# Softmax row sums in spare PSUM columns of the score banks, and a score bank that is refilled after the reciprocals instead of after the exponentials

## The reference, cut to what matters

```
x  = x + attention(groupnorm(x))
xn = layernorm(...)                                   # per position, 32 channels
scores = einsum('biqhd,bikhd->bihqk', q, k) + tri_bias + mask_bias    # 96 rows i, 4 heads, 96x96
a  = softmax(scores, axis=-1)
o  = einsum('bihqk,bikhd->biqhd', a, v)
out = einsum('bijk,ck->bijc', o * sigmoid(...), wo) + bo
```

## Time and profile before

| | |
|---|---|
| median of three runs | 320.16 us |
| the profiled execution | 320.25 us |
| its span (first to last record) | 318.4 us, so 1.85 us lie around it |
| PE busy, share of the span | 248.8 us (78%) |
| DVE busy | 241.3 us (76%) |
| ACT busy | 218.5 us (69%) |
| POOL busy | 128.0 us (40%) |
| attention pipeline | about 59 to 226 us of the span |

### The profile page before, as it was taken

One profiled execution on the slowest core, in us unless ns is written; L12 is line 12 of the kernel. 1 busy time (PEld: TensorE's weight loads), 2 busy tenths in 40 slices (PEclk: granted clock), 3 DMA queues, 4 the chain that ended last, 5 costly groups with the idle time before them and its releaser, 6 DMA issues.

```text
span 318.4 us, 7162 instructions
## 1 busy us (share of the span) xinstructions
PE 248.8 (78%) x2296; PEld 200.1 (63%) x2296; DVE 241.3 (76%) x543; ACT 218.5 (69%) x986; POOL 128.0 (40%) x140
## 2 busy tenths in 40 slices
PE   0597750589999999999999999998755977758710
PEld 0587320467778777887788787776555656658710
DVE  6058950578899888998989988887349479968994
ACT  1546650399998999998999989997445755426700
POOL 6670000045455455544554454555000365630562
PEclk9999595599999999999999999999758799978775
DMA  9100132635344354433544333410000462000017
GB/s 140 32 0 2 50 71 35 234 138 198 125 162 155 106 185 165 152 128 130 182 151 171 128 127 123 146 38 2 2 0 0 170 250 78 3 0 2 0 21 127
DMA packets 44041, 31.29 MB, mean 98 GB/s; under 512 B 23108, under 2 KB 44004, under 8 KB 44004
## 3 DMA queue, kind: packets, MB, share of 16 engines
q1 hardware_dynamic: 43004, 30.70, 30.5%
q10 hardware_dynamic: 1000, 0.13, 0.3%
HBM read 1.38 MB, written 1.18 MB: 8 GB/s over the span
## 4 chain that ended last, share of the span: by engine, by line
PE 64%; DVE 15%; DMA 6%; ACT 5%; issue 5%; SPq 2%; DVEq 0%; ACTq 0%
PE psum L1083 10%; PE psum L1135 10%; PE psum L1146 9%; PE psum L1086 5%; PE psum L1084 5%; PE psum L1115 5%; DMA maps<-mask_parts 4%; DVE tok L781 3%; PE psum L1001 3%; PE psum L979 2%; PE psum L1103 2%; PE psum L1204 2%; PE psum L1123 2%; DVE tok L836 2%; DMA maps<-in_x 2%
## 5 line engine op out<-in xcount | busy, mean ns | idle before, releaser
L497 POOL TENSOR_TENSOR probs<-probs,rden 96x384 f32<-96x384 f32 x96 | 79.0, 823 | 122.4 <-DVE rden L919 122.4
L645 ACT ACTIVATE probs<-psum,neg_max 96x96 f32<-96x96 f32 x384 | 124.1, 348 | 2.4 <-PE psum L1135 0.5
L645 ACT ACTIVATION_READ_ACCUMULATOR probs<-psum,neg_max 96x1 f32 x384 | 82.5, 215 | 0.0
L913 DVE COPY probs_t<-psum 96x384 f32<-96x384 f32 x96 | 52.9, 551 | 20.2 <-PE psum L1135 18.8
L882 DVE TENSOR_REDUCE neg_max<-psum 96x4 f32<-96x384 f32 x96 | 50.8, 529 | 2.0 <-PE psum L1086 2.0
L1083 PE MATMUL psum<-u_st,x_stack 128*96 128x384 f32 x96 | 40.5, 422 | 14.5 <-DMA u_st<-u_split 13.8
L1135 PE MATMUL psum<-ident,probs 96*96 96x96 f32 x384 | 47.7, 246 | 1.1 <-DVE probs_t L913 0.9
L1135 PEld LDWEIGHTS psum<-ident,probs 96*96 96x96 f32 x384 | 37.7, 126 | 5.4 <-issue 1.4
L1146 PE MATMUL psum<-probs_t,v_sb 128*32 128x96 f32 x768 | 35.8, 258 | 0.0
L1083 PEld LDWEIGHTS psum<-u_st,x_stack 128*96 128x96 f32 x96 | 15.7, 164 | 28.2 <-issue 14.0
L1086 PE MATMUL psum<-bias_lo,ident_r 128*96 128x384 f32 x96 | 33.0, 343 | 0.0
(11 more groups left out here) (167 smaller groups left out, 492.9 us busy)
## 6 DMA issues: line engine op xcount, KB each, us to landing
u_st<-u_split SPq DMA_DIRECT2D x96, 192.0 KB
x_stack<-shared SPq DMA_DIRECT2D x40, 96.0 KB, 2.1
x_stack<-bias_lo SPq DMA_DIRECT2D x10, 192.0 KB, 2.3
x_stack<-u_st SPq DMA_DIRECT2D x10, 192.0 KB, 2.3
maps<-in_x SPq DMA_DIRECT2D x4, 288.0 KB, 5.4
out_y<-maps SPq DMA_DIRECT2D x12, 96.0 KB, 2.2
x_stack<-shared SPq DMA_DIRECT2D x4, 192.0 KB, 2.3
bias_lo<-maps SPq DMA_DIRECT2D x24, 12.0 KB
```

Source lines behind the costliest of these rows:

```text
L497: pool.tensor_tensor(probs[:, m % SLOTS], probs[:, m % SLOTS], rden[:, m, :].unsqueeze(2).to_broadcast([N, H, N]), ALU.mult).then_inc(prob ...
L645: e = act.activation(probs[:, m % SLOTS, h], bank_s[m % 4][0:N, h * N:(h + 1) * N], ACT.Exp, bias=neg_max[:, m, h:h + 1], accum_out=den[:, ...
L913: dve.tensor_copy(probs_t[0:N, (m - T_BEHIND) % 2].rearrange("p h q -> p (h q)"), bank_t[0:N, 0:H * N]).then_inc(t_ready, 1)
```

## The change

`den` goes away. The row sums of row m are written to the four columns behind the scores, 384 to 387, of the same PSUM bank, and the reciprocals read them there. Since the bank now holds the row sums too, new scores may go into it only when the reciprocals of its last row are done, so PE waits for `rden_ready` where it waited for `exp_done`. The same count is used in the wait of the raw transposes behind the loop.

```diff
-        den = sb("den", [N, BODY, H])
...
+        def den_of(m):
+
+            return bank_s[m % 4][0:N, H * N:H * N + H]
...
-                                       ACT.Exp, bias=neg_max[:, m, h:h + 1], accum_out=den[:, m, h:h + 1])
+                                       ACT.Exp, bias=neg_max[:, m, h:h + 1],
+                                       accum_out=den_of(m)[:, h:h + 1])
...
-                    dve.reciprocal(rden[:, at, :], den[:, at, :]).then_inc(rden_ready, 1)
+                    dve.reciprocal(rden[:, at, :], den_of(at)).then_inc(rden_ready, 1)
...
-                need(pe, exp_done, BODY * r + m - 3)
+                need(pe, rden_ready, BODY * r + m - 3)
...
-                    pe.wait_ge(exp_done, s - 3)
+                    pe.wait_ge(rden_ready, s - 3)
```

## The result

The change makes the kernel slower: 365.83 us, the median of four executions (365.58 to 372.61), against 320.61 us in the same comparison. The ratio is 1.142 with a 95% interval of 1.137 to 1.146. The forecast was 367 us in a range of 361 to 378. Medians here are over all executions of a kernel, ratios over those near its fastest. The profiled execution took 365.63 us with a span of 363.8 us; its counterpart before took 320.25 us.

A forecast was written before the change was run, and what follows sets the result against it. PE was taken to pace the attention loop; the new wait makes PE and DVE take turns, 8.77 us per four steps against 6.70. 320.25 + 46.3 (loop) + 0.3 (start) = 366.9, stated as 367 us, range 361 to 378.

The forecast's parts named there:

- Piece 1: On PE, scores' start to transposes' start: 0.91, 1.48, 0.60, 0.78 us for n=0 to 3, together 3.77 per four steps.
- piece 4: Reciprocals' start to the start of whoever waits for them: 0.24 us, seen on POOL and taken for PE too.
- Pieces 2 and 3: PE transposes' start to DVE copy's start, 0.54 us, then copy's start to reciprocals' start, 0.47 us.
- The rival of the slow release: PE starts 0.15 us after DVE's end instead of 0.08, with a slower PSUM read: 373 to 379 us; chance 17%.
- The group: Four steps of the attention loop: 3.77 + 4 x 1.25 = 8.77 us against 6.70 before.
- The sum: 89 steps from the seventh scores take 195.1 us against 148.8, +46.3; with the start's +0.3 the total is 366.9 us.
- DVE at n=0: The tightest place: DVE's other work puts the copy 1.45 us behind the reciprocal, wanted at 1.69, so 0.24 us left.
- the ring: In the changed loop PE and DVE take turns: PE scores, extras, transposes; DVE copy, reciprocals; PE scores again; 0.52 us more per step.
- The row sums in PSUM: Reciprocals reading PSUM: no difference, bounds 0.02 us less to 0.06 more each; ACT's accumulator writes there: zero effect.
- The start: The seventh scores wait for the third reciprocals and move from 66.86 to 67.18 us: +0.32.
- The clock: Clock stays at 1.00 in the loop; as a rival, the whole loop at 1.2 GHz, +84 us, 451 us; chance 4%.
- the three cases that are slower by more than 0.5%: Forecast as worked out, 361 to 372 us, 77%; slow release of PE, 17%; fall of the clock, 4%.

The follow-up runs named there:

- three fillers behind the reciprocals: The changed kernel with three tiny DVE reciprocals into unused cells per step, right behind the row's reciprocals: 370.58 us.
- The fillers: The changed kernel with one, two or three tiny DVE reciprocals into unused cells per step, ahead of the row's reciprocals: 419.36, 417.36 and 470.89 us.
- one filler: The changed kernel with one tiny DVE reciprocal per step ahead of the row's reciprocals: median 419.36 us, executions 372.09, 412.56, 426.17, 469.65.
- two fillers: The changed kernel with two tiny DVE reciprocals per step ahead of the row's reciprocals: median 417.36 us, executions 376.61, 376.87, 457.85, 476.99.

## Why the prediction was right

**What bounds the kernel, and what is late.** Right. The reciprocals were late at all four places of a group, and PE waits for them 91 times.

**Piece 1, scores to transposes.** Right. In the change 131.15-129.67 = 1.48 at n=1 and 133.05-132.48 = 0.57 at n=2, against 1.48 and 0.60. The 0.03 less at n=2 goes with the 0.09 more of piece 4 there.

**Pieces 2 and 3.** 0.54 and 0.47, as taken from the earlier trace rows.

**Piece 4.** 0.24 was taken from POOL; PE needs 0.23, or 0.32 at n=2. The rival of the slow release, 0.31 at each step, is ruled out.

**The group.** 8.77 forecast. From 129.67 to 138.44 it is 8.77, over the loop 8.73. The sum said 195.1 for the 89 steps and 194.2 were measured. Behind the last scores nothing is added, as forecast: 102.8 us to the end of the span against 102.7.

**DVE at n=0.** It is in time, as forecast: that copy comes 1.69 us behind its reciprocal (136.06 to 137.75), and DVE has finished before. With three fillers behind the reciprocals the ring kept its pace in the profiled execution.

**The row sums in PSUM.** I took no difference for the reciprocals. They last 169 ns at the median where they lasted 164, so 0.005 and not 0.06, though of the two rows behind the choice one reads six columns and not one. ACT's half of it I had left open. The reads take 184 ns on the mean where they take 202 with the same wait and the sums in SBUF, and they are worth nothing in the changed loop because ACT waits:

```profile
L648 ACT ACTIVATE probs<-psum,neg_max 96x96 f32<-96x96 f32 x384 | 114.2, 351 | 32.7 <-PE psum L1139 32.7
...
L648 ACT ACTIVATION_READ_ACCUMULATOR probs<-psum,neg_max 96x1 f32 x384 | 69.9, 184 | 0.0
```

The cost by the cycles of the Trainium skill ("VectorE: DVE Perf Modes", section on the TRN2 errata), 0.065 us for each reciprocal, is not seen for this shape: 0.005. The Trainium skill ("ScalarE: Activation LUTs", on the stages of an ACTIVATE) says of an ACTIVATE's destination that PSUM is the faster one; here the exponentials still go to SBUF and only the accumulator read changes its destination, and for that read the traces point the same way, 184 against 202 ns. To save time it would need a loop in which ACT paces; here PE paces before the change, and the ring after it.

**The start.** The sum had +0.32 us up to the seventh scores. In the span they even come 0.09 earlier (66.77 against 66.86), but that is in part the luck of this execution: the first scores, which no wait of the change can touch, already start 0.29 earlier (59.11 against 59.40). From the first to the seventh it takes 7.66 us against 7.46, so +0.20. With the wait alone it is +0.48, and ACT's shorter reads would account for the difference, which is argued and not shown. The 0.9 of the loop and the 0.4 here are the 1.3 us by which 366.9 was above the profiled 365.63.

**The clock.** It held, as forecast, with 4% given to its fall. The fillers show that the margin was thinner than that number sounds: 0.07 us more per step, and it fell in three of four executions. Nothing in the prediction's rows told these loops apart, so that it held was right but in part luck. What exactly decides the fall is open. PE's busy share alone doesn't separate the cases: the last window at the full clock above has 5.93 of 8 us, and so have two windows of the profile with one filler (104 to 112 and 120 to 128), in which the clock held through the loop. Behind the attention there is one with 2.51 of 4 in which it held.

**The chances.** They don't quite add up: the three cases that are slower by more than 0.5% have 77, 17 and 4, together 98, where the text says 97.

## What to carry to other kernels

Before a wait is moved to a later event, look up what the producing engine has queued in front of that event. Here a 0.16 us operation stood behind a copy that waited for the very engine that was to wait, and this closed a ring: 1.25 us from PE's transposes to its next scores, where 0.74 had been enough. Moving the short operation ahead of the blocked one took the whole loss back. And where an edit leaves TensorE waiting in every step, price the fall of its clock beside the wait: the same kernel can stand on both sides of it.

## What the runs showed of the hardware that was not expected

- The same program fell to half clock in some executions and not in others: 376.6 and 457.9 us with two fillers, and in one profile the clock went from 1.00 to 0.50 after 112 us of a uniform loop.
- Four more matmuls per row on the waiting engine made such a kernel 88 us faster, 470.89 to 382.65 us.
- An accumulator read to PSUM is about 20 ns shorter than one to SBUF in the same loop: on the mean 184 against 202 ns with the new wait, 196 against 219 with the reciprocals moved up. The rest of the step from 215 ns before to 184 came with the slower loop. It frees ACT: 103.62 us busy against 110.62 of 120, with PE pacing both and the reciprocals in the same place.
- At half clock the hand-over from PE to DVE grows as well: from the start of the four transposes to the start of the waiting copy it is 0.88 us instead of 0.54.
- A tiny DVE reciprocal (96x1) takes 127 to 142 ns but holds the next one back by 0.06 to 0.07 us only.
